# Tiles of 128 rows in the memory feed-forward and the grouped attention's projections, and weight scaling on GpSimd

## What is computed

```python
# L1 ffn, on h = layernorm(x), every row by itself
query = h @ Wq.T;  rq = query @ Wr.T;  rk = aux_keys @ Wr.T
router = rq @ rk.T / sqrt(48) + log_rel;  top 8 of 256 slots
w = softmax((query @ sel_keys.T) / 8 + log_rel[sel]);  aux = (w @ sel_vals) @ Wvd.T @ Wvu.T
x = x + tanh(g) * (h + gate(h, gelu(h @ Wu1.T + bu1) @ Wu2.T) * aux)
# L2 xattn, 32 heads of 32, 8 key/value heads
q = (layernorm(x) @ Wq);  k, v = ctx @ Wk, ctx @ Wv
out = softmax(q k.T / sqrt(32)) v per batch and head;  x = x + tanh(g) * (out @ Wo)
# L2 ffn's weights, quantised: scale = max(max|w| over a row / 7, 1e-8); clip(round(w / scale), -8, 7)
```

## Time and profile before

| | |
|---|---|
| median of 3 runs | 2962.68 us (2954.92 to 2966.06) |
| the profiled execution's own time | 2972.02 us |
| its span | 2970.4 us |
| memory feed-forward | about 1369.9 to 1491.9 us of the span |
| grouped attention | about 1491.9 to 2182 us |
| PE / PEld / DVE / ACT / POOL busy | 2681.3 / 1856.6 / 1951.3 / 1071.0 / 451.2 us |

### The profile page before, as it was taken

One profiled execution on the slowest core, in us unless ns is written; L12 is line 12 of the kernel. 1 busy time (PEld: TensorE's weight loads), 2 busy tenths in 40 slices (PEclk: granted clock), 3 DMA queues, 4 the chain that ended last, 5 costly groups with the idle time before them and its releaser, 6 DMA issues. The chain is left out here.

```text
span 2970.4 us, 50445 instructions
## 1 busy us (share of the span) xinstructions
PE 2681.3 (90%) x18990; PEld 1856.6 (63%) x18994; DVE 1951.3 (66%) x3482; ACT 1071.0 (36%) x2425; POOL 451.2 (15%) x514
## 2 busy tenths in 40 slices
PE   7999999999998489997878999999877999878898
PEld 4665665766755288885645555555557888656664
DVE  5546546455452877665667878778637888967774
ACT  2433433333323333321323444444435555312222
POOL 0110101101101210000002222222212332300000
PEclk9999999999999789997878999999989999988999
DMA  6110101101100655555374445555160001434421
GB/s 261 49 35 14 36 13 48 36 13 48 36 6 18 241 164 138 149 149 163 115 226 140 146 142 160 167 161 147 43 214 16 23 23 44 121 122 178 172 89 38
DMA packets 153848, 304.70 MB, mean 103 GB/s; under 512 B 84017, under 2 KB 107217, under 8 KB 144137
## 3 DMA queue, kind: packets, MB, share of 16 engines
q1 hardware_dynamic: 127144, 229.90, 24.0%
q0 software_dynamic: 19376, 57.14, 6.5%
q10 hardware_dynamic: 7120, 15.01, 1.8%
HBM read 246.37 MB, written 43.04 MB: 97 GB/s over the span
## 5 line engine op out<-in xcount | busy, mean ns | idle before, releaser
L1958 POOL TENSOR_SCALAR grouped_probs<-grouped_probs,grouped_rsum 112x375 f32<-112x375 f32 x256 | 159.4, 640 | 623.7 <-DVE grouped_rsum L2009 623.7
L1572 DVE TENSOR_REDUCE latent_nmax<-bank 112x1 f32<-112x487 f32 x128 | 85.1, 665 | 246.7 <-PE bank L1437 239.2
L2214 PE MATMUL bank<-ffn_qT,gather_whole 128*128 128x128 bf16 x3584 | 209.3, 221 | 17.9 <-DVE ffn_gs L2458 6.7
L2214 PEld LDWEIGHTS bank<-ffn_qT,gather_whole 128*128 128x128 fp8e4 x3584 | 205.4, 99 | 22.6 <-issue 21.3
L1920 ACT ACTIVATE grouped_probs<-bank,grouped_nmax 112x375 f32<-112x375 f32 x256 | 143.1, 572 | 135.0 <-DVE grouped_nmax L2005 135.0
L1360 POOL TENSOR_SCALAR latent_probs<-latent_probs,latent_rsum 112x487 f32<-112x487 f32 x128 | 87.8, 686 | 637.7 <-DVE latent_rsum L1577 637.7
L1397 PEld LDWEIGHTS bank<-latent_hT,latent_wq 128*128 128x128 f32 x1536 | 175.3, 192 | 7.3 <-issue 7.1
L1397 PE MATMUL bank<-latent_hT,latent_wq 128*128 128x112 f32 x1536 | 175.1, 275 | 0.0
L2397 POOL TENSOR_TENSOR ffn_h<-ffn_sl,ffn_us 128x512 f32<-128x512 f32 x56 | 126.3, 2257 | 282.3 <-ACTq L2340 282.3
L1375 PE MATMUL bank<-latent_wv,latent_hT 128*125 128x384 f32 (+1 forms) x512 | 168.7, 491 | 0.0
L1426 PE MATMUL bank<-latent_wo,latent_oT 128*112 128x512 f32 x384 | 167.4, 592 | 0.0
(11 more groups left out here) (417 smaller groups left out, 5457.5 us busy)
## 6 DMA issues: line engine op xcount, KB each, us to landing
grouped_raw<-L_weights SPq DMA_DIRECT2D x24, 2048.0 KB, 8.5
points_spread<-numbers SPq DMA_DIRECT2D x16, 912.0 KB
codes<-grouped_flip SPq DMA_DIRECT2D x24, 512.0 KB, 2.6
latent_hT<-ctxT SPq DMA_DIRECT2D x8, 1500.0 KB
plain_ctxT<-ctxT POOLq DMA_DIRECT2D x8, 1500.0 KB
plain_ctx<-ctx POOLq DMA_DIRECT2D x8, 1500.0 KB
grouped_ctx<-ctxT SPq DMA_DIRECT2D x8, 1500.0 KB, 7.7
gather_whole<-numbers SPq DMA_DIRECT2D x12, 912.0 KB
```

The costliest lines, as they stand in the source:

```text
L1958: pool.tensor_scalar(pr[:, g % 2, j, :], pr[:, g % 2, j, :], rsum[:, g % 2, j:j + 1], 1.0, ALU.mult, ALU.mult)\
L2214: mm = pe.matmul(ahead.tile(t)[:, i * P:(i + 1) * P], wgu[:, u0 + f // 4, c:c + 2 * P - 1:2], qT[:, k, :], start=(k == 0), stop=(k == KC - 1))
```

## The change

Three things are changed.

1. **`memory_ffn`** reads and writes x as 7 tiles of 128 rows (896 / 128) in groups of 2, 2, 2 and 1 tile. A pair has 256 moving columns, the last group 128.
2. **`grouped_attention`**: z, q and the result x are 7 tiles of 128 rows; keys, values, scores and probabilities stay per batch. Tile n holds the last 112 - 16n rows of batch n and the first 16 + 16n of batch n+1. ScalarE therefore splits each copy of transposed queries in two (`queries`), and each output copy into `oT` in two, except for the first and the last batch. `qT` and `oT` have three slots in place of two. y of tile n runs in batch n+2 in place of n+1, so batch 1 has no y; tile n is still projected in batch n-1, so batch 6 has no query work. 
3. **Weights on GpSimd**: the four multiply-adds of `scaled` leave VectorE. GpSimd does them (`multiplied(u)`) after its probabilities of r = 2, 5, 7, once `rscale_ready` says that the reciprocals are there; each rounding on VectorE waits for its own quarter (`raw_scaled`).

The descriptor space of GpSimd's transfers is halved to 8192 bytes of a partition (`dynamic_dma_scratch_size`), which makes room for the larger tiles.

```diff
@@ memory_ffn
+    GROUPS = (TILES + 1) // 2
+    x_in, x_out = token_tiles(x_in), token_tiles(x_out)
+    def size(p):
+        return min(2, TILES - 2 * p)
-                for k in range(KC):
-                    mm = pe.matmul(turns.tile(t)[0:BOT, 0:2 * Q], wqT[:, k, :], zT[:, k, :], start=(k == 0), stop=(k == KC - 1))
+                n = size(p) * P
+                for k in range(KC):
+                    mm = pe.matmul(turns.tile(t)[0:BOT, 0:n], wqT[:, k, :], zT[:, k, 0:n], start=(k == 0), stop=(k == KC - 1))
...
-            for p in range(PAIRS):
-                more = p + 1 < PAIRS
+            for p in range(GROUPS):
+                more = p + 1 < GROUPS
...
@@ grouped_attention
-            n = b - 1 if name[0] == "y" else b + 1
-            if not 0 <= n < B:
+            n = b - 2 if name[0] == "y" else b + 1
+            if not 0 <= n < (B if name[0] in "kv" else TILES):
...
-                        chunks(t, item, lambda k: zT[:, k, :], lambda k: wq[:, k, i * 512:(i + 1) * 512], Q, 512)
+                        chunks(t, item, lambda k: zT[:, k, :], lambda k: wq[:, k, i * 512:(i + 1) * 512], P, 512)
...
-                        pe.wait_ge(oT_ready, QUADS * (n + 1))
-                        chunks(t, item, lambda k: oT[:, n % 2, k, :], lambda k: wo[:, k, i * 512:(i + 1) * 512], Q, 512)
+                        pe.wait_ge(oT_ready, QUADS * (n + 2))
+                        chunks(t, item, lambda k: oT[:, n % 3, k, :], lambda k: wo[:, k, i * 512:(i + 1) * 512], P, 512)
...
+            def queries(n):
+                here = Q - 16 * n
+                for h in range(2):
+                    t = ("qT", n, h)
+                    src = turns.tile(t)[:].rearrange("p (k q) -> p k q", k=4)
+                    act.wait_ge(turns.full(t), turns.count(t, 0))
+                    act.activation(qT[:, n % 3, 4 * h:4 * h + 4, Q - here:Q], src[:, :, 0:here], ACT.Copy)
+                    act.activation(qT[:, (n + 1) % 3, 4 * h:4 * h + 4, 0:P - here], src[:, :, here:P], ACT.Copy).then_inc(turns.free(t), 1)
+                act.drain().then_inc(qT_ready, 1)
...
-            for g in range(N):
-                pool.wait_ge(sum_ready, g + 1)
+            def multiplied(u):
+                slot, m = u % 2, 4 if u % 3 < 2 else 1
+                pool.wait_ge(rscale_ready, u + 1)
+                for i in range(4):
+                    w = raw[:, slot, i * D:(i + 1) * D]
+                    pool.tensor_scalar(w, w, rscale[:, slot, i % m:i % m + 1], MAGIC, ALU.mult, ALU.add).then_inc(raw_scaled, 1)
+
+            for g in range(BEGIN, N):
...
+                b, r = g // QUADS, g % QUADS
+                if r in (2, 5, 7):
+                    u = 3 * b + {2: 3, 5: 4, 7: 5}[r]
+                    if 0 <= u < UNITS:
+                        multiplied(u)
...
                 dve.reciprocal(rs, sc)
-                dve.drain()
-                for i in range(4):
-                    w = raw[:, slot, i * D:(i + 1) * D]
-                    dve.tensor_scalar(w, w, rscale[:, slot, i % m:i % m + 1], MAGIC, ALU.mult, ALU.add)
-                dve.drain()
+                dve.drain().then_inc(rscale_ready, 1)
 
             def rounding(u, i):
+                dve.wait_ge(raw_scaled, 4 * u + i + 1)
...
-                if r in (2, 3) and 1 <= b <= B:
-                    result(b - 1, r - 2)
+                if r in (2, 3) and 2 <= b <= B:
+                    result(b - 2, r - 2)
```

More of the change, by code:

```diff
@@ L903, in _ @@
                 sp.dma_start(dst[:], src).then_inc(key_loaded, 16)
-            for b in range(4, B):
+            for b in range(4, TILES):
                 load(b)
@@ L922, in turned @@
             def turned(p):
-                for s in range(2):
+                for s in range(size(p)):
                     pe.wait_ge(z_ready, p * 2 + (s + 1))
@@ L971, in mean_log @@
                 pe.wait_ge(turns.free("lsum"), turns.count("lsum", 0))
-                pe.matmul(turns.tile("lsum")[0:Q, 0:1], ones[:], lsum[:], start=True, stop=True).then_inc(turns.full("lsum"), 1)
+                pe.matmul(turns.tile("lsum")[0:P, 0:1], ones[:], lsum[:], start=True, stop=True).then_inc(turns.full("lsum"), 1)
             def routes(p):
@@ L991, in scores @@
                 pe.wait_ge(turns.free(t), turns.count(t, 0))
-                for s in range(2):
+                for s in range(size(p)):
                     for c in range(2):
-                        mm = pe.matmul(turns.tile(t)[0:Q, s:s + 1], hidT[:, i, c, s * Q:(s + 1) * Q], wu2[:, c:c + 1],
+                        mm = pe.matmul(turns.tile(t)[0:P, s:s + 1], hidT[:, i, c, s * P:(s + 1) * P], wu2[:, c:c + 1],
                                        start=(c == 0), stop=(c == 1))
@@ L1215, in one_over_one_plus @@
                 dve.drain()
-            for p in range(PAIRS):
-                for s in range(2):
+            for p in range(GROUPS):
+                n = size(p)
+                for s in range(n):
                     routed(p, s)
```

224 lines of the change are left out of this document (121 added, 103 removed).

## The result

The changed kernel took 2939.2 us (median of 5 runs, 2929.7 to 2947.0), the kernel before 2965.6 (5 runs of the same comparison, 2954.9 to 2969.7): a ratio of 0.9913, with a 95% interval of 0.9893 to 0.9932, or 26 us. The forecast was 2941 within 2925 to 2957. The sum came out, but not by its terms: a term that was sized too small and one that was sized too large made up for each other.

A forecast was written before the change was run, and what follows sets the result against it. TensorE sets the pace, with the path of rounding, transpose and store of codes, measurement and copies close under it. Terms -5 + 0 + 0 - 6 + 1 - 7.9 - 3.7 = -21.6 us gave 2941 from the median 2962.7; range 2925 to 2957.

The forecast's parts named there:

- The sum: Whole kernel: all terms together -21.6 us, so 2941 us from the median, at 0.55.
- Memory feed-forward: Memory block: three larger groups +6 us, single-tile last group -7.3, step before it -3.7; sum -5, between -9 and +1.
- Batch 0 and its lead-in: Grouped attention's start: VectorE earlier, but the measurement waits for a transfer; 0 us, between -2.7 and +1.
- Batch 1: Grouped attention without y: the 13.8 us of y bring nothing; 0, between -10 and +2; sign: near 79 us.
- Batches 2 to 5: Grouped attention, VectorE relieved: waits at r = 0 and 3 shrink, longer copies cost; -1.5 us each, -6 for four.
- Batch 6: Grouped attention without query work: waits, transposes and some of q's 13.8 us gained; -7.9 us, between -4 and -16.
- the clock rival: Batches 1 and 6: TensorE idles and then runs at 1.2 GHz; in batch 6 2 to 4 us; no chance given.
- Batch 7: Grouped attention's last batch: the 5.95 us wait shrinks by 2.7 and slow matmuls by about 1; -3.7 us.
- GpSimd: Grouped attention: scalings on GpSimd cost 1117 ns a quarter, 4.5 us a unit, and stay hidden.
- the first rival: Path through stores of codes holds the measurement in batches 2 to 5 too; -11 us, 2952; chance 0.27.
- TensorE's work gained in full: Whole kernel: all removed y, q, transposes and waits are gained; -52 us, 2911; chance 0.08.
- GpSimd as the bound: Grouped attention: slow scalings delay probabilities, gain gone from d = 3.0 us a quarter; +105 us, 3068; chance 0.05.

The follow-up runs named there:

- GpSimd alone: The kernel before with the multiply-adds on GpSimd and nothing else: 2949.2 us, 0.9941 of the kernel before.

## Why the prediction was right

*The sum* was right to 5 us (21.6 forecast, 26.3 measured), and its terms less so. Two errors met: the memory feed-forward brought 11 us for 5, batches 2 to 5 brought 2 for 6. That the medians agree to 2 us (2941, 2939.2) is luck besides: the kernel before took 2965.6 us in the comparison, 2.9 more than the 2962.7 that the sum began with. Of the signs, batch 1, the measurement's wait for the scales and the scalings' time came; 77 us a batch did not (81.2 to 77.2), nor 112 us for the memory block in this execution.

*Memory feed-forward.* The count of work was right, 4 to 7 us without the full clock. The mis-sized term is the query's: the clock of its 5.02 us was taken for fixed ("+0.7" a group), and in three of eight executions each of the first two queries fell by 1.3 us and more instead, and with them what runs around them. The alternative stood in the rows: 5.02 and 3.24 us for the same query. The prediction also read 5.02 as 1.2 GHz; at a granted clock of 0.64 it was a mix. And a projection of half the columns did take about half at full clock (1.96 us for 3.67, where the single tile's query had it), which the prediction did not count.

*Batch 0 and its lead-in.* 0, and the measurement does wait for a transfer, 3.11 us for 1.36. The 2.1 us that batch 0 won belong to the memory block. The premise that batch 0 takes as long as a batch with y came from a stretch that wasn't the batch (see the profile after); that the path through the store lies close under TensorE was true all the same.

*Batch 1.* Right, and the sign named came: 81.3 us without y, with TensorE waiting 8.64 us for the copies of r = 2. The forecast start of the measurement, 3.2 us behind the scales' issue, held as well (3.35, from 1623.62 to 1626.97). But it wasn't the only cause: with that wait gone, batch 1 still takes 78.1 us.

*Batches 2 to 5.* This is the step that failed: "it can be 1.6 us earlier, not 2.14". I read the room of the measurement off one batch, with its transpose of 10.54 us and 13.1 to the scales, the fastest of five. Batch 1 of the same trace shows 12.26 and 15.3; in the changed kernel the transposes at this place took 11.0 to 12.7. By the slower pace there is no room, and TensorE's wait only moved from r = 0 to r = 2. In batch 2 it was followed by half clock, and there the gain turned into a loss; in batches 3 to 5 it wasn't. GpSimd alone kept the gain in batches 1 to 3 and lost most of it in 4 and 5 (78.2 and 78.8 us, for 79.1 at full clock before). Its VectorE was ready in batch 2 as early as here (16.4 and 16.5 us behind the first scores), and the transfer landed 16.8 us behind the transpose's issue instead of 19.2. Why it was later in the changed kernel no run shows.

*Batch 6.* 5.7 us for 7.9. The term that was too large is that of r = 4 and 5: from the maxima of r = 4 to those of r = 6 it took 18.6 us, for a forecast of 16.5 and 20.3 before. TensorE waits 2.70 and 3.29 us for the copies there, and four transposes behind the second wait take 1.18 us for 0.69, v0 4.65 for 3.72; the clock rival had its cost at 2 to 4.

*Batch 7.* Right: from the scores of its first quad to those of its last it takes 47.5 us for 50.9, 3.5 less for 3.7. Another 1.6 us came behind, where I had nothing.

*GpSimd.* Nearly hidden: 1.12 us a quarter by the median; TensorE waits for its probabilities five times for 5.0 us in all (five times for 3.1 before), VectorE's roundings three times for 3.5, all ahead of batch 0. Two signs named for "wrong" thus came in small: these three, and TensorE's wait at r = 1 of batch 0, 3.05 us where it was 1.41.

The two engines do cost each other something: the 96 roundings took 74.3 us for 67.5, the 96 scalings 112.7 for 107.7 at their median. The prediction took 0.3 us for a part of one wait, and left open whether one engine is slowed or stopped. The trace decides it. A rounding that begins beside a scaling, and the scaling that is issued beside that rounding:

```profile
1691.49 1.12 POOL L1996 TENSOR_SCALAR grouped_raw<-grouped_raw,grouped_rscale 128x1024 f32<-128x1024 f32 x1
...
1692.21 0.94 DVE L2036 TENSOR_SCALAR mem_wu1T<-grouped_raw 128x1024 fp8e4<-128x1024 f32 x1
...
1692.58 1.55 POOL L1996 TENSOR_SCALAR grouped_raw<-grouped_raw,grouped_rscale 128x1024 f32<-128x1024 f32 x1
```

The first scaling ends at 1692.61 and the rounding 0.55 us later, at 1693.15; the second scaling ends 0.98 us after that. In this trace 34 roundings began more than 0.15 us before the end of a running GpSimd instruction. Of these 31 ended 0.55 us behind that end, whatever was left of it, and 3 took their usual 0.69 to 0.70 us while the scaling took 1.65; none lies between. So here one stands still until the other is through. The Trainium skill ("SBUF — State Buffer", "SBUF: two separate sides") has it so where VectorE works in one of its two-port modes: the one that starts first has the shared ports for its whole instruction, and the other is blocked. The trace agrees. The cost is small since a rounding mostly begins when only 0.2 to 0.5 us of a scaling are left: 6.8 us over 96 roundings. What this costs the kernel, for which the prediction set 4 us beside its sum, no run separates.

*The rivals.* The second bound took most of the gain in batches 2 to 5, as the first rival said, and with the third all of batch 1's; its 5.8 us for batch 6 is nearer than the forecast's 7.9. Of the 13 us that it is short, 5.8 lie in the memory block, 6.7 in batches 0 to 5 and 1.3 in batch 7. TensorE's work gained in full was wrong by three bounds, one behind the other. GpSimd as the bound needs d of about 2.5 us, and it has 1.12.

## What to carry to other kernels

When a wait of the bounding engine is taken away, follow the chain behind it over every batch of the trace and take the longest of its transfers, not one: a room of 1.6 us with transfers that scatter by 2 to 3 is no room. Ask why a wait on a store exists at all: here what it guarded in the measurement was 16 bytes a partition, and two more places for them were worth 19 us once VectorE was relieved, as much as either part of the change alone, and 5 to 6 before. And work taken off an engine at a step where it waits for another brings nothing; moving other work into that step does.
